# Three cross attentions of one kernel: the subtracted maximum in three bf16 parts, scores one step further ahead, PSUM sums copied before the division

## The reference, cut to what matters

```
# x: (4, 512, 128), context: (4, 77, 128), 16 heads of 8
q = heads(layernorm(x) @ Wq.T + bq);  k, v = heads(ctx @ Wk.T + bk), heads(ctx @ Wv.T + bv)
s = (q k^T * tau + delta) / sqrt(8)
x = x + (softmax(s, axis=-1) @ v) @ Wo.T + bo
...
x = x + L0_xcond(...); x = x + L0_ffn(...)      # mixture of experts
x = x + L1_xcond(...); x = x + L1_ffn(...)      # convolution MLP
x = x + L2_xcond(...); x = x + L2_ffn(...)      # six layers of local attention
x = x + L3_xcond(...); x = x + L3_ffn(...)      # mixture of experts
```

## Time and profile before

| what | us |
|---|---|
| time, median of 3 runs | 2585.14 (2583.83 to 2594.27) |
| span of the profiled execution, first to last instruction | 2576.0 |
| TensorE busy in it | 2259.8 (88%) |
| VectorE busy | 1921.9 (75%) |
| ScalarE busy | 1237.9 (48%) |
| GpSimd busy | 1161.5 (45%) |
| mean granted clock of TensorE | 0.934 |

### The profile page before, as it was taken

How to read it: one execution, slowest core, us unless ns; L and a number is a source line. 1 busy time by engine, 2 the same in 40 slices (tenths; PEclk the granted TensorE clock), 3 DMA queues, 4 the chain that set the end, 5 groups by cost and what they waited for, 6 DMA issues and landing times.

```text
span 2576.0 us, 83743 instructions
## 1 busy us (share of the span) xinstructions
PE 2259.8 (88%) x36496; PEld 1557.8 (60%) x36496; DVE 1921.9 (75%) x4241; ACT 1237.9 (48%) x2267; POOL 1161.5 (45%) x854
## 2 busy tenths in 40 slices
PE   6959768975999999999999999999999999878675
PEld 3537634443666766666766666766766666645464
DVE  4553366667998888988898989898988989555612
ACT  2423233333556555565565565656565565334231
POOL 1025410004665655665565656665666556310064
PEclk9969978887999999999999999999999999889787
DMA  7101100001111111112111211121111011220012
GB/s 245 66 18 35 50 23 1 1 1 28 36 32 35 36 50 41 31 35 65 43 31 33 67 27 31 35 65 35 40 35 31 23 40 31 52 84 6 13 35 75
DMA packets 62105, 107.09 MB, mean 42 GB/s; under 512 B 11604, under 2 KB 46687, under 8 KB 55212
## 3 DMA queue, kind: packets, MB, share of 16 engines
q1 hardware_dynamic: 57004, 93.45, 12.9%
q0 software_dynamic: 4736, 8.29, 1.5%
HBM read 42.70 MB, written 13.24 MB: 22 GB/s over the span
## 4 chain that ended last, share of the span: by engine, by line
PE 64%; DVE 15%; issue 9%; POOL 9%; ACT 2%; DMA 1%; SPq 1%; POOLq 0%; DVEq 0%; ACTq 0%
PE ps L2013 9%; PE ps L2116 5%; PE ps L2095 5%; PE ps L2034 4%; POOL mem L2730 4%; PE ps L2022 4%; PE ps L2057 4%; PE ps L2072 3%; PE ps L2175 3%; PE ps L2161 2%; PE ps L2152 2%; PE ps L1039 2%; POOL mem L2743 2%; PE ps L559 2%; PE ps L1519 2%
## 5 line engine op out<-in xcount | busy, mean ns | idle before, releaser
L2730 POOL TENSOR_TENSOR mem<-mem 128x512 f32<-128x512 f32 x384 | 572.7, 1499 | 582.2 <-DVE mem L2290 579.0
L2013 PE MATMUL ps<-mem 128*128 128x512 f32 x768 | 383.4, 612 | 4.3 <-DVE mem L2290 2.0
L2569 ACT ACTIVATE mem<-ps 128x512 f32<-128x512 f32 x384 | 222.1, 604 | 158.0 <-PE ps L2034 157.4
L2548 ACT ACTIVATE mem<-ps 128x512 f32<-128x512 f32 x384 | 220.6, 598 | 126.9 <-PE ps L2013 86.8
L2285 DVE TENSOR_TENSOR mem<-ps,mem 128x512 f32<-128x512 f32 x384 | 258.7, 674 | 22.8 <-ACT mem L2548 22.4
L2290 DVE TENSOR_TENSOR mem<-ps,mem 128x512 f32<-128x512 f32 x384 | 261.1, 680 | 0.0
L2034 PEld LDWEIGHTS ps<-mem 128*128 128x128 f32 x1536 | 187.7, 145 | 109.7 <-issue 95.8
L2095 PEld LDWEIGHTS ps<-mem 64*64 64x64 f32 x12288 | 195.3, 137 | 83.8 <-issue 83.5
L2297 DVE TENSOR_REDUCE mem<-mem 128x16 f32<-128x1024 f32 x192 | 231.9, 1208 | 0.0
L2743 POOL TENSOR_TENSOR mem<-mem 128x1024 f32<-128x1024 f32 x96 | 182.3, 1899 | 96.2 <-DVE mem L2359 96.2
L2095 PE MATMUL ps<-mem 64*64 64x32 f32 x12288 | 208.0, 222 | 12.8 <-issue 10.5
(11 more groups left out here) (294 smaller groups left out, 4173.0 us busy)
## 6 DMA issues: line engine op xcount, KB each, us to landing
mem<-mem SPq DMA_DIRECT2D x48, 768.0 KB, 5.8
mem<-in_Wqkv SPq DMA_DIRECT2D x6, 1536.0 KB, 6.8
mem<-mem SPq DMA_DIRECT2D x36, 256.0 KB, 3.5
y<-mem SPq DMA_DIRECT2D x8, 512.0 KB, 6.4
mem<-in_W12T SPq DMA_DIRECT2D x8, 512.0 KB, 7.7
mem<-y SPq DMA_DIRECT2D x16, 256.0 KB, 4.7
mem<-in_L3W SPq DMA_DIRECT2D x16, 256.0 KB, 5.8
mem<-in_L2Wo SPq DMA_DIRECT2D x6, 512.0 KB, 7.0
```

Source lines behind the costliest of these rows:

```text
L2013: e.matmul(self.K.ps[:, o, :], self.columns(u, bb), self.K.l2[l % 2]["Wqkv"][:, 512 * i:512 * i + 512], start=True, stop=True, skip_group_ ...
L2569: e.activation(to, view(self.K.ps[:, self.FEATURE[i], :], "p (c q) -> p c q", c=4), ACT.Copy).then_inc(s("placed"), 1)
L2730: e.tensor_tensor(t1[:, cols], t1[:, cols], self.T2[:, cols], ALU.add).then_inc(s("rotated"), 1)
```

## The change

Six things change in `CrossAttention`, and two around it:

1. **The maximum in three parts.** `v_max` writes to a small tile `mx`, and a new `v_parts` splits the four maxima of a step into three bf16 numbers each (cast, subtract, cast, subtract, each waiting for the one before). `pe_turn_max` turns them with bf16 matmuls against a bf16 identity, `mT` is bf16, and the second half of `pe_less` multiplies bf16 `pickb` with bf16 `mT`. The 32 rows of a group hold 4 heads times 3 parts.
2. **Scores further ahead.** Scores 0 and 1 of step w+2 are computed in step w; before, all four of step w+1 were.
3. **A copy out of PSUM.** ScalarE copies bank 6 to `sums` (`a_sums`); reciprocal and product read `sums`, and `pe_weigh` waits for the copy, not for the division.
4. **Order.** The projection of a step is one step later; the rows of a new batch are turned at the start of an even step, behind its first `pe_less`, and no longer late in it; `v_prepare` comes one step earlier.
5. **Portions.** VectorE's side work is played out in portions of 3, 1, 1 and 3 a step, and the rest at the end of each odd step; before, it was 3 or 6 behind each maximum, 1 and 3 around the division, and the rest in the first round of each even step.
6. `identb` is cast at the start of the program; `pick` is loaded as bf16.

```diff
@@ tensor @@
-        for q in range(self.NQ + 3):
-            w, rd = divmod(q, 2)
...
+        self.pe_score(e, 1, 0)
+        self.pe_score(e, 1, 1)
+        for w in range(self.NW + 1):
+            batch, next, next2 = w % 2 == 0 and w // 2 + 1 < B, w + 1 < self.NW, w + 2 < self.NW
+            if w < self.NW:
+                self.pe_less(e, 2 * w)
             if batch:
-                self.pe_queries(e, q // 4 + 1)
...
+                self.pe_turn_rows(e, w // 2 + 1)
+            if next:
+                self.pe_score(e, w + 1, 2)
+            if w >= 1:
+                self.pe_weigh(e, 2 * w - 1)
+            if batch:
+                self.pe_queries(e, w // 2 + 1)
+            if next:
+                self.pe_score(e, w + 1, 3)
+            if w < self.NW:
+                self.pe_less(e, 2 * w + 1)
+            if w >= 2:
+                self.pe_project(e, w - 2)
+            if next2:
+                self.pe_score(e, w + 2, 0)
+            if w < self.NW:
+                self.pe_weigh(e, 2 * w)
+            if next:
                 self.pe_turn_max(e, w + 1)
+            if next2:
+                self.pe_score(e, w + 2, 1)
+        self.pe_project(e, self.NW - 1)
@@ pe_turn_max, pe_less, pe_weigh @@
-            last = e.transpose(K.ps[:, 7, 128 * t:128 * t + 128], self.mx[w % 2][:, t, :], K.ident)
+            last = e.matmul(K.ps[:, 7, 128 * t:128 * t + 128], self.parts[w % 2][:, t, :], K.identb, start=True, stop=True,
+                            skip_group_check=True)
...
-                last = e.matmul(K.ps[0:L, 2 + j, 256 * x:256 * x + 256], K.pick[p, i, :], self.mT[w % 2][p, :], start=False,
+                last = e.matmul(K.ps[0:L, 2 + j, 256 * x:256 * x + 256], K.pickb[p, i, :], self.mT[w % 2][p, :], start=False,
...
-            e.wait_ge(*s.at("att", w))
+            e.wait_ge(*s.at("sums", w))
@@ vector @@
+        for w in range(self.NW + 1):
+            next, next2 = w + 1 < self.NW, w + 2 < self.NW
+            if w % 2 == 0 and w // 2 + 2 < B:
+                self.v_prepare(e, w // 2 + 2)
...
+            if next:
+                self.v_max(e, w + 1, 2)
+                self.fill(3)
+                self.v_max(e, w + 1, 3)
+                self.v_parts(e, w + 1)
+            if w >= 2:
+                self.v_add(e, w - 2)
+            if next2:
+                self.v_max(e, w + 2, 0)
+                self.fill(1)
+            if w >= 1:
+                self.v_divide(e, w - 1)
+            if next2:
+                self.v_max(e, w + 2, 1)
                 self.fill(3)
-            if q % 4 == 0:
+            if w % 2 == 1:
                 self.fill(99)
@@ scalar @@
+        for w in range(self.NW):
+            batch = w % 2 == 0 and w // 2 + 1 < B
+            self.a_exp(e, 2 * w, 0)
+            self.a_exp(e, 2 * w, 1)
             if batch:
...
+                self.a_cols(e, w // 2 + 1)
+            self.a_exp(e, 2 * w, 2)
+            self.a_exp(e, 2 * w, 3)
+            if batch:
+                self.a_queries(e, w // 2 + 1)
+            if w:
+                self.a_sums(e, w - 1)
+            self.a_exp(e, 2 * w + 1, 0)
...
+                self.a_max(e, w + 1)
+        self.a_sums(e, self.NW - 1)
...
+    def a_sums(self, e, w):
+        s = self.s
+        if w:
+            e.wait_ge(*s.at("att", w))
+        e.wait_ge(*s.at("weighed", 2 * w + 2))
+        e.activation(self.sums, self.K.ps[:, 6, :], ACT.Copy).then_inc(s("sums"), 1)
```

More of the change, by code:

```diff
@@ L416, in __init__ @@
         self.qT = tile3(2, S)
[L417 to L418 removed]
+        self.mx, self.rest = (tile4(2, 4, 4) for _ in range(2))
+        self.parts = [view(words(128).bitcast(BF16), "p (t c) -> p t c", t=2) for _ in range(2)]
+        self.mT = [words(128).bitcast(BF16) for _ in range(2)]
         self.rcp = words(256)
         self.oT = words(256)
+        self.sums = words(512)
         if pt_where:
@@ L600, in vector @@
             self.fill(4)
+        self.v_parts(e, 0)
+        for k in range(2):
+            self.v_max(e, 1, k)
+            self.fill(4)
         self.fill(99)
-        for q in range(self.NQ + 3):
-            w, rd = divmod(q, 2)
-            if rd == 0 and w % 2 == 1 and w // 2 + 2 < B:
+        for w in range(self.NW + 1):
+            next, next2 = w + 1 < self.NW, w + 2 < self.NW
+            if w % 2 == 0 and w // 2 + 2 < B:
                 self.v_prepare(e, w // 2 + 2)
-            if self.last and q == self.NQ - 2:
+            if self.last and w == self.NW - 1:
@@ L624, in vector, with v_add @@
                 self.fill(3)
-            if q % 4 == 0:
+            if w % 2 == 1:
                 self.fill(99)
-            if q == 0 and self.beside:
+            if w == 0 and self.beside:
                 self.extra = chain(self.extra, self.beside.v_steps(e))
+        self.v_add(e, self.NW - 1)
         self.fill(999)
+    def v_add(self, e, w):
+        K, s = self.K, self.s
+        e.wait_ge(*s.at("projected", w + 1))
+        if w % 2 == 0:
+            e.wait_ge(*s.at("row_bias", w // 2 + 1))
+        X = K.X[:, 2 * w:2 * w + 2, :]
+        e.tensor_tensor(X, X, view(K.ps[:, 7, 0:256], "p (a c) -> p a c", a=2), ALU.add).then_inc(s("added"), 1)
+        if self.norms and w % 2 == 1:
+            self.extra = chain(self.extra, self.norms(e, w // 2, s.at("added", w + 1)))
```

118 lines of the change are left out of this document (51 added, 67 removed).

## The result

The changed kernel takes 2597.8 us (median of 19 runs, 2589.8 to 2616.3) beside 2582.0 us for the kernel before in the same rounds: a ratio of 1.0070, 95% interval 1.0057 to 1.0083. It is 0.7% slower, 14 us over the forecast of 2583.7: inside the range, but the forecast was of no change. In a second set of rounds the ratio was 1.0046 (1.0020 to 1.0073). By these ratios the change costs 12 to 18 us, where the prediction had a saving of 1.4: for the change itself the miss is 13 to 20 us. The profiled execution took 2611.9 us, 14 above the median, with a span of 2610.1.

The account below looks back on a forecast made before the run. TensorE was taken to set the pace, VectorE adding stalls. The attentions' terms, -2.4, +3.1 and -2.1, sum to -1.4: span 2574.6 against 2576.0, with 9.1 outside 2583.7 us, no measurable change; range 2556 to 2608.

Parts of the forecast that it names:

- pe_less, turned maximum, unstalled step: Odd step on TensorE: `pe_less` from 1.79 to 1.27 us, turned maximum about 0.07 less, step without stall 9.83.
- v_parts and VectorE's chain: Before the turned maximum: four dependent VectorE instructions take 0.88 us; with them VectorE just keeps the 9.83 us step.
- nothing left over: VectorE's chain in a step: parts, addition and division just fit; each further 0.1 us costs 0.1 a step.
- a_sums: ScalarE's copy out of PSUM takes 0.6 us, costs 0 in the loop, lies on the path in the tail.
- The waits for side work: TensorE stalls in steps 2, 4, 6: 2.6, 3.5, 2.35 us in first and third attention; 9.4, 6.35, 5.2 in second.
- Start: First `pe_less` of each attention waits for side work, parts and two more scores: net +1 us each, 0 to 3.
- Tail: Last step's `pe_less` to last addition: 16.7 us, +2 in first and third attention, +0.3 in second.
- The clock: Half clock behind the new waits, nine in all: 5.5 us each in first and third attention, 9 in second.
- clock lost at its upper end: Rival, shared with a longer VectorE chain: half clock costs up to 11 us each attention, 2597 to 2605 us; chance 0.12.
- what would show it: Signs in the new trace: `pe_less` 1.2 to 1.3 us, odd steps 9.9, nine waits, half clock, second attention no shorter than 90.

## Why the prediction was wrong, point by point

*pe_less, turned maximum, unstalled step: right.* 1.37 for 1.27 (inside its ends), 0.16 saved for 0.07, and 9.85 for 9.83.

*v_parts and VectorE's chain: right.* Four instructions take 0.85 (88.05 to 88.90) for 0.88, and the chain keeps up: with the side work dealt out, steps of 9.73 have no wait. It had more room than "nothing left over": in that kernel 11 and more side instructions a step fit beside the chain's own eleven (22 to 27 instructions in each of steps 2 to 5 of the first attention).

*a_sums: right.* 0.60 us, hidden in the loop, and worth far more than its cost.

*The waits for side work: right.* Predicted for the first attention 2.6, 2.45 with 1.05, and 2.35; measured 2.48, 2.28 with 0.97, and 2.22 (2.28 with 0.97 where the clock stayed full). In step 6 of the second 5.2 was predicted and 5.32 measured. Steps 1 to 6 without clock come to 221.6 by the run that kept TensorE busy, for 224.8.

*Start: too low.* I had +1 each. The first `pe_less` of the first attention starts at 40.85 instead of 37.69, +3.2, a little above the upper end of 3 that I gave: the two further scores are then done, but ahead of the turned maximum stands a wait of 3.8 for the parts. Counted from the end of the stage ahead, it is 2.6 to 4.3 later in the other two attentions. With TensorE kept busy it comes to 9 us in all three, 6 more than I had; in the first, 0.8 of it is won back by the start of step 1.

*Tail: right with TensorE kept busy.* From the last step's first `pe_less` to the end of the last addition I had 16.7; with TensorE kept busy it is 17.0 (125.05 to 142.03), in the changed kernel itself 20.2 (134.16 to 154.35), 18.1 in its second trace, for 14.7 in the earlier trace rows. So it is 2.3 longer there, and 3.4 to 5.5 in the changed kernel.

*The clock: this step failed.* I put 2 us on each of the stretches, 3 in the second attention, 5.5 + 5.5 + 9 = 20 in all, from one stretch of 7.4 us. Measured, from the end of the stage ahead to the attention's last addition, the changed kernel against the one with TensorE kept busy: 12.3, 19.2 and 7.4 us in its first trace, 8.0, 14.9 and 8.3 in the second, 31 to 39 in all. By the medians it is 31 to 37. The 11 to 19 us over my 20 are the larger part of the miss; the 6 at the start are the rest of it that has a row, and the steps give 3 back. What I had wrong is the length: each wait was given one stretch like that of the earlier trace rows, and they are 10.1, 6.9 and 17.1 us in the first attention, 54.7 and 17.0 in the second, 10.2 and 13.6 in the third. The second trace has the same: its steps 2, 3 and 4 of the second attention are 26.05, 17.72 and 19.70. My rows were also read too narrowly. The prediction says that a wait of 1.03 cost nothing and that nothing lies between it and 2.34. The second attention before has waits of 1.34 and 1.67, both followed by full clock, and one of 1.03 that was followed by 6.8 us of half clock (step 3, granted clock 0.90). In both traces of the kernel before that attention has more half clock than the others (0.91 and 0.84 against 0.94 to 0.96), and all that I gave it for this was 3 us a stretch instead of 2. (The 4.43 of the earlier trace rows is the idle time of the weight loads; TensorE's own there is 3.96.) Of the rivals it is the last, with 0.12, by its second half: "clock lost at its upper end", 2597 to 2605. The upper end was 11 us for each attention; the first lost 8 to 12, the second 15 to 19, the third 7 to 8.

Of "what would show it" the odd steps, the waits with their releasers, the half clock behind them and the second attention over 90 us came. Of the nine waits one, in step 4 of the third attention, had no half clock behind it in either trace. The slot is 1.37, a little over 1.2 to 1.3. The first attention at 75 to 77 us and the tail 2 us longer did not come: 79.4 and 77.4 in the two traces, and 5.5 and 3.4 for the tail, where with TensorE kept busy it is 2.3.

Open are three things. Why a wait of 2.28 is answered once with half clock and three times not. Why in the second attention the clock stays at half although TensorE works from 393.6 to 424.9 without a wait; in the other steps of this kernel it came back within 17 us. And the way from the second attention's last addition to the third's first `pe_less`, which takes 1837.9 and 1837.4 us (before), 1852.8 and 1851.0 us (after) and 1838.4 with TensorE kept busy in the attentions. Three to four of these 14 us are the third attention's start; the others lie in code that did not change (1826.8 and 1826.3 before, 1837.4 and 1837.1 after, 1824.4 kept busy), with the same granted clock of 0.97 in each. That the change makes them is only a guess, since no row names it.

## What to carry to other kernels

Side work that fills an engine's gaps has to be dealt out by the length of the gaps: played in one piece "where it must be done", it turned a gain of 1.8% into a loss of 0.5 to 0.7%, with every instruction the same. A new wait of TensorE of 2 us and more is to be priced by the work that runs at half clock behind it, here 7 to 19 us an attention, and not by its own length; a shorter one, of 1.0 to 1.8 us, was mostly free and sometimes not. And a saving on the busiest engine is measured only once its waits are gone: the bf16 parts were worth nothing, or less, in two orders, and 21 us in the third.

## What the runs showed of the hardware

Useless matmuls made the kernel faster: two of 512 columns, 2.0 us of work in a wait of 2.5, kept the granted clock at 1.00 in a step where it had been 0.73, and with some thirty of them the kernel gained 31 to 37 us.

Waits of TensorE in steps 1 to 6 and the clock behind them, where it was full ahead of the wait. Half clock followed each of the six waits of 2.48, the one of 3.03 and all six of 2.22 and 2.23 (four in the changed kernel, two with the rows turned late). It followed one of the four of 2.28 and 2.29; one of 1.50 and one of 1.80 (steps at 0.79 and 0.80); four of the eight of 1.58 to 1.78 with the fp32 maximum; two of the eight of 1.67 and 1.68 with the parts alone; in the kernel before one of the two of 1.34, three of the fourteen of 1.03, and not the one of 1.67. With TensorE kept busy in its longer waits, 2.03 and 1.70 were followed by full clock. So were, in all eight traces of the changed order with the parts, the 3.8 us ahead of the first turned maximum of the first attention. Length alone does not decide.

In steps 1 to 6 of the changed kernel half clock lasted 6.8 to 17.1 us, but for the second attention, where one stretch lasted some 55 in both traces. With the parts alone one lasted 27.3, again in the second attention, and TensorE was busy in 26.9 of it.

Eight of the sixteen matmuls of 256 columns of a `pe_less` (16 of its 32 records) in bf16 instead of fp32 shorten it from 1.79 to 1.37 us, 0.05 for each.
